# A two-layer graph network on one core: the norm's row statistics move from VectorE to ScalarE, an addition to GpSimd, and the bias matmul goes from fp32 to bf16 parts

## The reference

```python
def _layernorm(x, axis=-1, eps=1e-05):
    m = jnp.mean(x, axis=axis, keepdims=True)
    v = jnp.var(x, axis=axis, keepdims=True)
    return (x - m) / jnp.sqrt(v + eps)

# layer 0: attention over the row's neighbours, 8 heads, q from x, k and v given
scores = jnp.einsum('hnd,hmd->hnm', q, k)
scores = jnp.where(adj > 0, scores, NEG_FILL)
out0 = jnp.einsum('hnm,hmd->hnd', softmax(scores), vv)
x = _layernorm(x + out0)

# layer 1: graph attention
h = (x @ W_w.T + W_b).reshape(Bn, H, D)
e = jax.nn.leaky_relu(s_src[:, None, :] + s_dst[None, :, :], negative_slope=0.2)
e = jnp.where(adj[:, :, None] == 0, jnp.float32(-1000000000.0), e)
h_prime = jnp.einsum('ijh,jhd->ihd', softmax(e, axis=1), h)
x = _layernorm(x + jax.nn.elu(h_prime))
```

## Time and profile before

| | us |
|---|---|
| median of 3 runs | 498.96 |
| lowest and highest | 497.28, 499.59 |
| the profiled execution | 500.55 |
| its span | 498.9 |
| mean granted TensorE clock in it | 0.714 |

### The profile page before, as it was taken

The page is one execution under the profiler, slowest core; times in us unless marked ns, Lnnn a source line. Parts: engine busy times, 40 slices in busy tenths (PEclk is TensorE's granted clock), DMA queues, the critical chain, the costliest instruction groups (busy, mean ns, idle before and its releaser), DMA issues.

```text
span 498.9 us, 5673 instructions
## 1 busy us (share of the span) xinstructions
PE 277.4 (56%) x1506; PEld 193.7 (39%) x1506; DVE 314.6 (63%) x870; ACT 157.2 (32%) x352; POOL 239.6 (48%) x383
## 2 busy tenths in 40 slices
PE   0338676447755865886898875230004535595680
PEld 0226443335433543654556543120003423373450
DVE  3997988999978996996836620300014345677773
ACT  6433745325343334233221222000010022535322
POOL 7453746572478574478461335777742726000000
PEclk9859785969566995797755975575555957676796
DMA  8886567275277233154022002444431424101001
GB/s 308 266 266 233 213 206 262 57 284 169 97 198 228 109 88 107 43 135 125 1 68 84 12 24 67 112 112 112 112 78 28 113 60 109 45 1 43 21 1 47
DMA packets 24484, 57.94 MB, mean 116 GB/s; under 512 B 6560, under 2 KB 14880, under 8 KB 22400
## 3 DMA queue, kind: packets, MB, share of 16 engines
q0 software_dynamic: 10032, 31.77, 22.9%
q1 hardware_dynamic: 14416, 25.76, 14.9%
HBM read 53.19 MB, written 4.33 MB: 115 GB/s over the span
## 4 chain that ended last, share of the span: by engine, by line
PE 20%; another core or an unknown queue 16%; DVE 12%; issue 7%; POOL 3%; ACT 3%; DVEq 0%; ACTq 0%; POOLq 0%
PE e_po L1313 10%; PE e_pj L1328 2%; DVE e_weighted L1566 2%; PE e_pj L1326 1%; PE e_po L1297 1%; ACT e_sel_edges L1109 1%; DVE e_stats L1342 1%; PE e_pt L1222 1%; PE e_pq L1257 1%; POOL e_ring L965 1%; DVE e_y L1352 1%; DVE e_y L1589 1%; DVE e_y L1587 1%; POOL e_rstd L983 1%
## 5 line engine op out<-in xcount | busy, mean ns | idle before, releaser
L1313 PE MATMUL e_po<-e_weighted,e_sel_edges 128*128 128x264 f32 x312 | 100.9, 483 | 17.1 <-DVE e_weighted L1566 13.7
L965 POOL DMA_INDIRECT e_ring<-table,e_col_i x78 | 74.0, 948 | 45.2 <-DVE e_weighted L1566 22.3
L965 POOL DMA_INDIRECT e_ring<-in_kv,e_col_i x78 | 77.9, 998 | 34.6 <-issue 20.6
L1313 PEld LDWEIGHTS e_po<-e_weighted,e_sel_edges 128*128 128x128 f32 x312 | 73.2, 243 | 38.9 <-DVE e_weighted L1566 19.3
L1109 ACT COPY e_sel_edges<-e_pt 128x512 f32<-128x512 f32 (+3 forms) x45 | 23.6, 524 | 98.2 <-remote 53.3
L1222 PE MATMUL e_pt<-e_identb,e_sel_rows 128*128 128x128 bf16 x156 | 21.4, 273 | 44.9 <-ACT e_sel_edges L1109 31.1
L1566 DVE TENSOR_TENSOR e_weighted<-e_ring,e_pc 128x528 f32<-128x528 f32 (+1 forms) x55 | 35.6, 684 | 14.6 <-PE e_po L1313 9.5
L1257 PE MATMUL e_pq<-e_parts,e_sel_rows 128*128 128x256 bf16 x234 | 43.7, 351 | 1.0 <-DVE e_prod L1510 1.0
L1297 PE MATMUL e_po<-e_mean_row,e_diagonal 128*128 128x264 f32 x64 | 24.4, 474 | 35.3 <-issue 21.4
L1381 DVE MAX8 e_raw<-e_vals 128x8 bf16<-128x256 bf16 (+1 forms) x88 | 41.5, 513 | 1.0
L1222 PEld LDWEIGHTS e_pt<-e_identb,e_sel_rows 128*128 128x128 bf16 x156 | 14.1, 120 | 54.3 <-issue 52.5
(11 more groups left out here) (184 smaller groups left out, 534.0 us busy)
## 6 DMA issues: line engine op xcount, KB each, us to landing
e_adj<-in_adj SPq DMA_DIRECT2D x16, 1024.0 KB
table<-e_hx SPq DMA_DIRECT2D x16, 136.0 KB
e_ring<-in_kv SPq DMA_DIRECT2D x1, 2112.0 KB, 13.1
out<-e_prod SPq DMA_DIRECT2D x16, 128.0 KB, 1.7
e_ring<-in_kv,e_col_i POOLq DMA_INDIRECT x78
e_ring<-table,e_col_i POOLq DMA_INDIRECT x78
e_xres<-in_x SPq DMA_DIRECT2D x2, 512.0 KB
e_xres<-in_x SPq DMA_DIRECT2D x3, 256.0 KB, 12.0
```

What stands on the lines that cost most here:

```text
L965: nc.gpsimd.indirect_dma_start(out=rings[layer][:, q % RING[layer], :], out_offset=None, in_=kv if layer == 0 else table, in_offset=bass.I ...
L1313: nc.tensor.matmul(po[n % 2][:, 0:CV], sel_edges[:, (layer * plan.n_chunks + q) % TURNED, :], weighted[:, b % 3, j * CV:(j + 1) * CV], sta ...
```

## The change

Layer 0: the addition of `x` goes from DVE to POOL (a new stage `add_x`); `bn_stats`, `bn_aggr` and the epsilon leave DVE. A new ACT stage `spread_of` takes the row sum times -1/C (Copy with an accumulator) and the sum of squares about the mean (Square with the mean as bias and an accumulator). POOL's `shift` now has three instructions, the epsilon first. Layer 1: DVE's addition of `x` becomes one instruction that also gives the row sum (`with_x`), and ACT gets `spread_of_b` (a 128x1 Copy and the Square). The bias matmul takes three rows of bf16 parts of the bias instead of one fp32 row; for them the bias is loaded to three partitions, and POOL splits it once in a new stage `split_b`. The costs in `all_stages` are changed to match, so stages move on all engines but SP. Cut to its core:

```diff
         if layer == 0:
-            put("DVE", 2.1, rank - 0.2, ("norm", k), end, ("x", plan.group_of_k(k)), ("normed", k - 4) if k >= 4 else None)
-            put("POOL", 1.1, rank - 0.3, ("shift", k), ("norm", k))
+            put("DVE", 0.75, rank - 0.2, ("norm", k), end, ("normed", k - 4) if k >= 4 else None)
+            put("POOL", 0.75, rank - 0.3, ("add_x", k), ("norm", k), ("x", plan.group_of_k(k)))
+            put("ACT", 1.4, rank - 0.3, ("spread_of", k), ("add_x", k), ("project", k - 2) if k >= 2 else None)
+            put("POOL", 1.4, rank - 0.3, ("shift", k), ("spread_of", k))
...
-            sp.dma_start(b_row[:, 0:CV].rearrange("p (h e) -> p h e", e=D1)[:, :, 0:D], w_b.rearrange("(a h d) -> a h d", a=1, d=D)).then_inc(s("w_loaded"), 16)
+            for p in range(3):
+                sp.dma_start(b_row[p:p + 1, 0:CV].rearrange("p (h e) -> p h e", e=D1)[:, :, 0:D], w_b.rearrange("(a h d) -> a h d", a=1, d=D)).then_inc(s("w_loaded"), 16)
...
+                    own.did(nc.gpsimd.tensor_scalar(var_eps[:, one], squares[:, one], 1.0 / C, EPS, ALU.mult, ALU.add))
+                    own.wait()
                     own.did(nc.gpsimd.tensor_tensor(rstd[:, one], var_eps[:, one], minus_half[:], ALU.pow))
                     own.wait()
-                    nc.gpsimd.tensor_scalar(shift[:, one], mv[:, k % 4, 0:1], rstd[:, one], -1.0, ALU.mult, ALU.mult).then_inc(s("shift_ready"), 1)
+                    nc.gpsimd.tensor_tensor(shift[:, one], neg_mean[:, one], rstd[:, one], ALU.mult).then_inc(s("shift_ready"), 1)
+                elif stage[0] == "add_x":
+                    k = stage[1]
+                    pool.wait_ge(s("sums_read"), k + 1)
+                    pool.wait_ge(x_loaded[plan.group_of_k(k)], 16)
+                    nc.gpsimd.tensor_tensor(y[:, k % 4, :], y[:, k % 4, :], xres[:, k, :], ALU.add).then_inc(s("z_ready"), 1)
+                elif stage[0] == "split_b":
+                    pool.wait_ge(s("w_ready"), 3)
+                    own.did(nc.gpsimd.tensor_scalar(less[:, 0:1], part_no[0:3, :], 0.5, -1.0, ALU.is_gt, ALU.mult))
+                    own.did(nc.gpsimd.tensor_scalar(less[:, 1:2], part_no[0:3, :], 1.5, -1.0, ALU.is_gt, ALU.mult))
+                    own.did(nc.gpsimd.memset(onesb, 1.0))
+                    for j in range(2):
+                        own.did(nc.gpsimd.tensor_copy(b_parts, b_row[:]))
...
+                elif stage[0] == "spread_of":
...
+                    own.did(nc.scalar.activation(xts[k % 2][:], y[:, k % 4, :], ACT.Copy, scale=-1.0 / C, accum_out=neg_mean[:, one]))
+                    own.wait()
+                    nc.scalar.activation(xts[k % 2][:], y[:, k % 4, :], ACT.Square, bias=neg_mean[:, one], accum_out=squares[:, one]).then_inc(s("var_ready"), 1)
+                    act.wait_ge(s("var_ready"), k + 1)
+                elif stage[0] == "spread_of_b":
...
+                    own.did(nc.scalar.activation(neg_mean[:, one], total[:, one], ACT.Copy, scale=-1.0 / C))
+                    own.wait()
+                    nc.scalar.activation(elu[:, k % 2, :], y[:, k % 4, :], ACT.Square, bias=neg_mean[:, one], accum_out=squares[:, one]).then_inc(s("var_ready"), 1)
...
-                    pe.wait_ge(s("w_loaded"), 16 * (6 + 2 * H))
+                    pe.wait_ge(s("w_loaded"), 16 * (8 + 2 * H))
...
-                    nc.tensor.matmul(pj[:, 0:CX], ones[0:1, :], b_row[:], start=True, stop=False)
+                    if k == 0:
+                        pe.wait_ge(s("bias_split"), 1)
+                    nc.tensor.matmul(pj[:, 0:CX], onesb, b_parts, start=True, stop=False)
...
+            def with_x(k):
+                return v.scalar_tensor_tensor(out=y[:, k % 4, :], in0=y[:, k % 4, :], scalar=1.0, in1=xres[:, k, :],
+                                              op0=ALU.mult, op1=ALU.add, accum_out=total[:, k % 4:k % 4 + 1])
...
-                    dve.wait_ge(x_loaded[plan.group_of_k(k)], 16)
-                    st.did(v.tensor_tensor(y[:, k % 4, :], y[:, k % 4, :], xres[:, k, :], ALU.add))
-                    st.wait()
-                    st.did(moments(k))
-                    st.wait()
-                    v.tensor_scalar(var_eps[:, k % 4:k % 4 + 1], mv[:, k % 4, 1:2], EPS, None, ALU.add).then_inc(s("var_ready"), 1)
...
-                    st.did(v.tensor_tensor(y[:, k % 4, :], y[:, k % 4, :], xres[:, k, :], ALU.add))
-                    st.wait()
-                    moments(k).then_inc(s("var_ready"), 1)
-                    dve.wait_ge(s("var_ready"), NT + k + 1)
+                    with_x(k).then_inc(s("z_ready"), 1)
```

52 lines of the change are left out of this document (35 added, 17 removed).

## The result

The changed kernel takes 480.36 us (median of 4 runs, 479.27 to 481.11), the one before 498.66 (4 runs): a ratio of 0.9633, interval 0.9603 to 0.9663. What lies outside the span grows from 1.65 to 3.2 us. Over all runs it is 2.4 to 3.5 us with the bf16 bias and 1.6 to 2.0 with the fp32 one, but for two runs of one kernel with 2.1 and 2.6; why is not shown.

A forecast was written before the change was run, and what follows sets the result against it. No engine's total was taken to bound the kernel, but four stretches: DVE's lists, PE's sums, POOL's gathers, DVE again. 500.55 - 7.5 + 7.0 - 4.4 - 2.5 = 493.15, less 1.6 gives 491.5 us; range 483 to 501.

The forecast's parts named there:

- term 2: Start: two more bias loads on SP at 2.98 us each delay sum_w, split_b adds 1; +7.0 us, bounds +1 and +10.
- term 4: Layer 1: gathers keep their length, then fifteen norms each free 0.5 us of DVE, a third credited; -2.5 us.
- term 3: From 205 to 304 us: cheaper bias matmul -5.0, last norm's longer latency +1.6, DVE time -1.0; -4.4 us.
- first rival, hidden loads: Start: added loads cost 0.5 us of SP each or DVE makes up the delay; 485.5 us, chance 0.22.
- Term 1: List stretch before 205 us: six layer-0 norms each free 1.41 us of busy DVE; -7.5 us, bounds 3 and 8.5.
- rival of the longer norm: After 205 us: project waits in each of ten tiles for a norm visiting POOL and ACT twice; 506 us, chance 0.13.
- Relief that turns into waiting: Before 205 us half of DVE's freed time becomes waits, layer 1 gains 0; 498 us, no change, chance 0.16.
- The bias not cheaper: Bias matmul: bf16 on three partitions takes as long as fp32 for some fixed cost; 496.5 us, chance 0.04.
- GpSimd's addition: Layer 0's norm: addition on POOL takes 773 ns against 510 on DVE, ratio 1.5; the skill's rule says about twice.

The follow-up runs named there:

- first setting: The first runs, both kernels unaltered: the kernel before at 498.66 us, the changed kernel at 480.36, ratio 0.9633.
- early dummies: Changed kernel plus two pairs of bn_stats and bn_aggr on a constant, on DVE behind the division of each of the first six tiles: 428.61 us, 0.984 of the kernel before.
- new order with the old work: Kernel before in all its instructions, with the changed kernel's order on every engine (new stages empty): 438.73 us, 1.0118 of the kernel before.
- second setting: Later comparisons, same kernels: the kernel before at 435.7 to 436.5 us, the changed kernel at 424.89 and 424.28, ratios 0.9751 and 0.9731.
- old order: Stages ordered as in the kernel before, new stages set in at fixed places; with all the changed kernel's work 459.91 us, 1.057 of the kernel before.
- the planner knows the waits only: Changed kernel's instructions, planner given the new stages and their waits but the old costs: 445.45 us, 1.0208 of the kernel before.

## Why the prediction was wrong, point by point

It forecast faster, rightly, and less than half of the gain. In the first setting the profiled executions differ by 21.3 us, where the sum had 7.4. The steps that failed are term 2 and term 4; a premise failed with them. Term by term the traces miss the sum by 5 at the start, by 3 in term 3 and by 8 in layer 1, and 1.5 us outside the span, taken as unchanged at 1.65, go the other way.

**Term 2, the start: +7.0 forecast, about +2 measured.** The step "the same form in the same place" took the row of the one b_row load, 2.98 us, for the price of each. Three took 4.50, so the further ones cost 0.76, near the lower bound of 0.4 and far from the upper. The split took 6.8 us, not 5, and delayed the flags by 1.9, so the +1 was the small part and should have been the large one. That is 5 us of the miss. The first rival, hidden loads, had this step right, and its 485.5 was the nearest of the cases. The other half of the step, that a delay of `sum_w` passes on whole, was not tried as a delay; an advance of 8.4 us brought the first division only 0.4 forward.

**Term 1, DVE in the list stretch: -7.5 forecast.** With a start 2 later and the seventh division 5.3 earlier, the trace gives -7.3. The size is right and, by the run with the early dummies, so is its reason: 8.1 us given back to DVE there put the seventh division off by 6.8. The new order with the old work brought it forward by 1.4 alone.

**Term 3, 205 to 304: -4.4 forecast, -7.1 measured, -4.1 in the second setting.** The bias is worth about 5, as said, and 4.5 in this stretch even in the old order. A bf16 bias matmul takes 0.36 us on the mean, not 0.15 to 0.27, but the path gained what it was given. The last norm is 0.8 us longer, not 1.6: the 0.3 for each hand-over between engines stood on no row, and the four hand-overs from the last division's end to the start of its normalised row took 0.03 to 0.09 us each. DVE's time there was rightly held cheap. Of the surplus of 2.7 in the first setting the runs say that it is not there in the second; the granted clock of the stretch was 0.74 before and 0.78 after in the first, 0.83 and 0.79 in the second, which goes the same way and was not tried apart.

**Term 4, layer 1: -2.5 forecast, -10.5 measured.** Here the most was lost, 8 us. The size of the relief was right: 1.035 us of DVE become 0.507 in each tile, 0.53 less, where the sum had 0.5; both prices were 0.09 too high. What failed is the weight, "of 15 x 0.5 = 7.5 I credit a third". In the second setting the new statistics gain 5 to 6 us in the new order for 8.4 us of DVE, about two thirds, and the stretch as a whole gains 4.6. Order decides here as well: in the old one the same statistics cost 6.4. The remaining 6 us belong to the first setting, and their cause is open. They do not come from a backlog that is worked off at full speed: between the second tile and the tenth, behind the longest of the late results, DVE is busy for 32.3 of 54 us before and 26.2 of 45 after, less densely than in the second setting (32.6 of 42, 26.1 of 37). So about the same relief of DVE, 6 us, shortens that part by 9 in one setting and by 5 in the other. The other reading that failed is "from 304 to 382 the gathers pace the kernel, one every 1.25 us". The earlier trace rows has a pause of 13.22 us in them and a wait of 26 for results that PE had finished 23 us before its end. In the second setting the gathers go on without a pause and the second tile's division comes 49 us after the first gather instead of 93. That part did keep its length between the two kernels, but for another reason than the one given: both have the late results.

**The premise, that order is neutral.** The forecast counted instructions taken and added, and treated the moved stages as nothing. The runs show that the gain hangs on them: the same work costs 24 us in the old order and 9 when the planner knows the waits only. The rival of the longer norm had POOL's queue in view, but the other way round: additions that stand behind gathers which wait for the ring. In the old order it is the additions that wait, for DVE, with gathers behind them, and half of their price is POOL's own added work. In the new order, in the second setting, POOL is idle for 102 us up to layer 1's first gather, where before it was 131, and its 19 us of added work fit into that. I gave the rival 0.13 without having looked at where the additions stand in the middle of layer 0.

**The rivals.** Relief that turns into waiting: not so before 205, nor in layer 1. The bias not cheaper: refuted, sixteen tiles take 5.8 us of PE instead of 15.5. GpSimd's addition: 742 ns against 455 for DVE's, a ratio of 1.6, and the version without it is 1 to 4 us faster. The advice of the Trainium skill, page "GPSIMD Engine Reference", section "4.1 Engine selection", to leave such an addition to VectorE, points the right way here, for a sum that is hardly clear of the noise.

## What to carry to other kernels

When costs in a planner change with the work, judge them together: the same instructions were 24 us slower or 11 us faster, by nothing but where they stood in the queues. Before a wait in the changed kernel is called the cause, look for it in the kernel before: POOL's 22 us at the additions had a forerunner of 25. Ask of a changed stretch how long it became, not only of the whole: the medians hid half of a gain of 5 us in layer 1 and a third of a loss of 7 in the list stretch. One load's issue took 2.98 us and the next of the same form 0.66; take a row's duration for a second one only when the trace shows a second one. And when a profile has long waits that nothing in it explains, forecast the stretch behind them with a wide margin, or as a case of its own.

## What was not expected of the hardware

- The kernel before took 498.7 us in the first runs and 435.7 to 436.5 in the five comparisons after. Only in the traces of the former are PE's results taken up late, by 23 us on DVE (328.05 to 351.47) and 32 on ACT (330.87 to 362.60). Cause open; whether it goes with the chip can't be said, as no record names the chip of the first runs.
- A one-row load of 1 KB to `e_b_row` held SP's queue for 2.98 us, two more of them for 1.5 together. Of the two `e_w_ext` loads it was the second that took 5.10 us, and 0.65 when it stood 7 us later in the queue.
- With the bf16 bias 2.4 to 3.5 us of an execution lie outside the span, with the fp32 bias mostly 1.6 to 2.0. Cause open.
- On DVE the addition with a row sum takes 425 ns for 128x256, exactly what the plain addition took, + 82 ns for the read; another instruction of the same form with other inputs took 517.
- ACT's Square with one per-row operand took 508 ns for 128x256, between the 416 of none and the 598 of two. The Trainium skill, page "ScalarE: Activation LUTs", section "What ACT_TABLE_LOAD costs", gives 93 ns for each such operand; the traces have 92 and 90.
